# The sums of the first query half: two key tiles added on GpSimd, one late product with ones, and a new order of small DMAs

## The reference

```
qkv = clip(xn @ Wqkv.T, -8, 8);  q, k = layer_norm(q), layer_norm(k)
scores = q k^T / sqrt(32) + slope[h] * (j - i), causal
out = softmax(scores) @ v @ Wout.T
ffn = xn @ (alpha * sign(W)).T + bias
```

## Time and profile before

| | us |
|---|---|
| median of 3 runs | 1409.92 (1408.61 to 1413.5) |
| profiled execution, its own time | 1414.06 |
| its span, first to last instruction | 1412.3 |
| TensorE busy | 1341.1 (95%) |
| VectorE busy | 791.2 (56%) |
| ScalarE busy | 512.0 (36%) |
| GpSimd busy | 446.0 (32%) |
| TensorE's granted clock, mean | 0.993 of full |

### The profile page before, as it was taken

One profiled execution on the slowest core, in us unless ns is written; L12 is line 12 of the kernel. 1 busy time (PEld: TensorE's weight loads), 2 busy tenths in 40 slices (PEclk: granted clock), 3 DMA queues, 4 the chain that ended last, 5 costly groups with the idle time before them and its releaser, 6 DMA issues.

```text
span 1412.3 us, 36370 instructions
## 1 busy us (share of the span) xinstructions
PE 1341.1 (95%) x15012; PEld 678.3 (48%) x15012; DVE 791.2 (56%) x1794; ACT 512.0 (36%) x1019; POOL 446.0 (32%) x313
## 2 busy tenths in 40 slices
PE   5799999999999999699999999989999999999998
PEld 2344444444454444244345555555555555444443
DVE  4677266655566661112578778878877788201111
ACT  5444111111111110000037767767777777700000
POOL 1222000000000000000005555555544445697665
PEclk9999999999999999899999999999999999999999
DMA  5445122223222225712122333332333332144543
GB/s 214 156 158 198 70 53 67 67 72 77 61 74 67 70 71 134 195 68 81 54 62 57 90 87 81 89 79 79 84 89 87 87 87 60 46 170 136 165 148 119
DMA packets 143799, 137.99 MB, mean 98 GB/s; under 512 B 81969, under 2 KB 110769, under 8 KB 143474
## 3 DMA queue, kind: packets, MB, share of 16 engines
q1 hardware_dynamic: 79199, 99.55, 23.3%
q10 hardware_dynamic: 64467, 36.50, 10.1%
HBM read 93.42 MB, written 42.21 MB: 96 GB/s over the span
## 4 chain that ended last, share of the span: by engine, by line
PE 77%; DMA 9%; DVE 6%; issue 3%; ACT 2%; SPq 2%; POOL 0%; DVEq 0%; ACTq 0%; POOLq 0%
PE ps L1029 49%; PE ps L1099 7%; PE ps L1160 6%; DMA arena<-arena 5%; PE ps L1183 5%; PE ps L1188 4%; DVE ps L931 2%; PE ps L1076 2%; PE ps L1163 1%; DMA arena<-q_scr 1%; SPq L357 1%; PE ps L1193 1%; DMA v_scr<-arena 1%; ACT arena L663 1%; PE ps L1018 1%
## 5 line engine op out<-in xcount | busy, mean ns | idle before, releaser
L1029 PE MATMUL ps<-arena 128*128 128x512 f16 x3584 | 792.7, 381 | 17.9 <-DVE arena L890 11.8
L1029 PEld LDWEIGHTS ps<-arena 128*128 128x128 f16 (+1 forms) x3584 | 348.8, 98 | 437.2 <-issue 17.3
L740 ACT ACTIVATE arena<-ps 128x512 f32<-128x512 f32 (+3 forms) x768 | 339.6, 498 | 146.0 <-PE ps L1163 92.9
L599 POOL TENSOR_TENSOR arena<-arena 128x2048 f32<-128x2048 f32 (+1 forms) x48 | 201.8, 4204 | 390.8 <-ACT arena L740 388.4
L931 DVE CUSTOM_DVE_ANT_0 ps<-ps,arena 128x128 f32<-128x128 f32 (+3 forms) x512 | 239.4, 518 | 58.2 <-PE ps L1099 56.0
L1160 PE MATMUL ps<-arena 128*32 128x512 f16 (+3 forms) x3072 | 255.3, 327 | 4.0 <-ACT arena L740 2.5
L1099 PE MATMUL ps<-arena 127*32 127x512 f16 (+3 forms) x3072 | 237.3, 327 | 14.7 <-DVE arena L931 10.2
L648 ACT ACTIVATE arena<-arena 128x512 f32 (+1 forms) x64 | 40.1, 629 | 492.2 <-DMA arena<-in_wqkv_t 317.0
L890 DVE TENSOR_SCALAR arena<-ps 128x1024 f32<-128x1024 f32 x48 | 58.8, 1225 | 216.9 <-PE ps L1029 187.6
L935 DVE TENSOR_REDUCE arena<-ps 128x1 f16<-128x512 f32 x256 | 162.9, 682 | 15.7 <-PE ps L1099 15.7
L1183 PE MATMUL ps<-arena 128*32 128x512 f32 (+3 forms) x1536 | 160.8, 485 | 0.5 <-issue 0.3
(11 more groups left out here) (53 smaller groups left out, 785.9 us busy)
## 6 DMA issues: line engine op xcount, KB each, us to landing
arena<-in_x SPq DMA_DIRECT2D x32, 512.0 KB, 5.3
arena<-in_wqkv_t SPq DMA_DIRECT2D x48, 256.0 KB, 2.9
arena<-k_scr ACTq DMA_DIRECT2D x39, 256.0 KB
base_scr<-arena SPq DMA_DIRECT2D x16, 512.0 KB, 2.9
v_scr<-arena SPq DMA_DIRECT2D x16, 512.0 KB, 2.9
arena<-r_scr SPq DMA_DIRECT2D x32, 256.0 KB
arena<-base_scr SPq DMA_DIRECT2D x16, 512.0 KB, 4.4
out_dram<-arena SPq DMA_DIRECT2D x16, 512.0 KB, 6.2
```

What stands on the lines that cost most here:

```text
L599: nc.gpsimd.tensor_tensor(acc[:, :, at:HALF], former, p32[k % PSLOTS][:, :, 0:w], ALU.add)\
L740: nc.scalar.activation(p32[k % PSLOTS][:, j, 0:w], ps[:, TRB[x % RB], 0:w], ACT.Exp, scale=SCALE).then_inc(exp_done, 1)
L1029: ins = nc.tensor.matmul(dst[c], lhs(k, a), wparts[:, k, b, c * HALF:(c + 1) * HALF], start=(k == 0 and (a, b) == order[0]), stop=(k == KT ...
```

## The change

Chunks 1 and 2 of each group lose their products with ones, and so does chunk 0. GpSimd adds the slots of chunks 1 and 2 into chunk 0's slot (`add_first`), once TensorE has multiplied chunk 0 with V. `sums_first`, after the third score set of chunk 6, multiplies that slot with ones; chunk 3 keeps its own product and opens the bank. Since chunk 0's slot is kept longer, the slots are given by a table (`SLOT`, with `HELD` for the chunk that had the slot before), and chunk 3 shares a slot with chunk 2, chunk 11 with chunk 10. The sums of the first half are copied on their own (`sums0_copy`). On SyncE the next group's maxima row goes ahead of the previous half's reciprocals. The reciprocals stand at items 18 and 33 instead of 22 and 32, the stack loads at chunks 1 to 8 and V's at chunk 9, and `NATS`, `PV_AFTER` and the places of `o_norm`, `o_low`, `o_high` have new numbers.

```diff
         st_done = sem("st_done")
         exp_done = sem("exp_done")
         add_done = sem("add_done")
+        add0_done = sem("add0_done")
+        sums0_done = sem("sums0_done")
         pv_done = sem("pv_done")
         o_out = sem("o_out")
         s_out = sem("s_out")
...
             at = max(0, P * t - HALF * qb)
             return qb, t, at, HALF - at
-        NATS = [3, 4, 3, 4, 2, 5, 3, 4, 5, 3, 3, 3]
+        NATS = [3, 4, 3, 4, 3, 4, 4, 4, 5, 3, 2, 3]
         assert sum(NATS) == ITEMS
-        PV_AFTER = {(0, 2): [-2], (2, 1): [-1], (3, 0): [0], (4, 2): [1], (5, 2): [2], (6, 2): [3],
+        PV_AFTER = {(0, 2): [-2], (2, 1): [-1], (3, 0): [0], (4, 2): [1], (5, 2): [2], (5, 3): [3],
...
         def due(c, j):
...
         ADDED = (1, 2, 3, 5)
-        DIRECT = [qb == 0 or t not in ADDED for qb, t in CHUNKS]
+        DIRECT = [t not in (ADDED if qb else (0, 1, 2)) for qb, t in CHUNKS]
         ADDS = len(ADDED) - 1
+        ADDS0 = 2
+        FIRST_ADDS = {3: [1, 2]}
+
+
+
+        SLOT = [(0, 0), (1, 0), (2, 0), (2, 2 * P), (3, 0), (1, 0), (2, 0), (0, 0), (3, 0), (1, 0), (2, 0), (2, 2 * P)]
+
+
+        HELD = [-5, -3, -2, -1, -4, 1, 3, 0, 4, 5, 6, 6]
+
+        def slot(c):
+            i, col = SLOT[c]
+            return p32[i][:, :, col:col + span(c)[3]]
         def adds_for(k):
             n, c = k // NC, k % NC
-            return 0 if DIRECT[c] else ADDS * n + max(1, ADDED.index(CHUNKS[c][1]))
+            return ADDS * n + max(1, ADDED.index(CHUNKS[c][1])) if CHUNKS[c] in [(1, t) for t in ADDED] else 0
+
+        def adds0_for(k):
+
+            n, c = k // NC, k % NC
+            return ADDS0 * n + min(c, ADDS0) if 0 < c <= QB_END[0] else 0
         V_FIRST = NT - 4
...
                 row_b_in(n)
                 if n > 0:
                     sums_out(blk_no(n - 1, 1))
-                    recips_in(blk_no(n - 1, 1))
                 if n < GROUPS - 1:
                     row_a_in(n + 1)
+                if n > 0:
+                    recips_in(blk_no(n - 1, 1))
                 sums_out(blk_no(n, 0))
                 recips_in(blk_no(n, 0))
...
                 if t == ADDED[1]:
                     need(pool, pv_done, n * NC)
                 need(pool, add_done, adds_for(k) - 1)
-                former = p32[(k - 1) % PSLOTS] if t == ADDED[1] else acc[:, :, at:HALF]
-                nc.gpsimd.tensor_tensor(acc[:, :, at:HALF], former, p32[k % PSLOTS][:, :, 0:w], ALU.add)\
-                  .then_inc(add_done, 1)
+                former = slot(c - 1) if t == ADDED[1] else acc[:, :, at:HALF]
+                nc.gpsimd.tensor_tensor(acc[:, :, at:HALF], former, slot(c), ALU.add).then_inc(add_done, 1)
+
+            def add_first(n, c):
+
+                at = span(c)[2]
+                k = n * NC + c
+                pool.wait_ge(exp_done, GH * (k + 1))
+                pool.wait_ge(pv_done, n * NC + 1)
+                need(pool, add0_done, adds0_for(k) - 1)
+                total = slot(0)[:, :, at:HALF]
+                nc.gpsimd.tensor_tensor(total, total, slot(c), ALU.add).then_inc(add0_done, 1)
             for n in range(GROUPS):
                 for c in range(NC):
-                    if not DIRECT[c] and CHUNKS[c][1] > ADDED[0]:
+                    if CHUNKS[c] in [(1, t) for t in ADDED[1:]]:
                         add_in(n, c)
+                    for first in FIRST_ADDS.get(c, []):
+                        add_first(n, first)
                     if n > 0:
-                        if c == 1:
+                        if c == 0:
                             o_norm(n - 1, 0)
-                        if c == 4:
+                        if c == 5:
                             o_low(n - 1, 0)
                         if c == 7:
                             o_norm(n - 1, 1)
...
                 x = GH * k + j
                 w = span(c)[3]
                 if j == 0:
-                    need(act, pv_done, k - PSLOTS + 1)
-                    need(act, add_done, adds_for(k - PSLOTS))
+                    former = n * NC + HELD[c]
+                    need(act, pv_done, former + 1)
+                    need(act, add_done, adds_for(former))
+                    need(act, add0_done, adds0_for(former))
+                    if c == SLOT[1:].index(SLOT[0]) + 1:
+                        act.wait_ge(sums0_done, n + 1)
                 act.wait_ge(st_done, x + 1)
-                nc.scalar.activation(p32[k % PSLOTS][:, j, 0:w], ps[:, TRB[x % RB], 0:w],
+                nc.scalar.activation(slot(c)[:, j, :], ps[:, TRB[x % RB], 0:w],
                                      ACT.Exp, scale=SCALE).then_inc(exp_done, 1)
             def os_copy(n, qb):
...
                 act.wait_ge(pv_done, n * NC + QB_END[qb] + 1)
                 need(act, ol_done, m - 1)
                 nc.scalar.activation(os_sb[m % 2][:, 0, :], ps[:, O_BANK, :], ACT.Copy).then_inc(o_out, 1)
-                nc.scalar.activation(os_sb[m % 2][:, 1, :], ps[:, S_BANK, :], ACT.Copy).then_inc(s_out, 1)
+                if qb == 1:
+                    nc.scalar.activation(os_sb[m % 2][:, 1, :], ps[:, S_BANK, :], ACT.Copy).then_inc(s_out, 1)
+
+            def sums0_copy(n):
+
+                act.wait_ge(sums0_done, n + 1)
+                nc.scalar.activation(os_sb[0][:, 1, :], ps[:, S_BANK, :], ACT.Copy).then_inc(s_out, 1)
             def o_high(n, qb):
...
                     for j in range(GH):
                         exps(n, c, j)
                         if n > 0:
-                            if (c, j) == (2, 0):
+                            if (c, j) == (2, 1):
                                 o_high(n - 1, 0)
                             if (c, j) == (2, 1):
                                 os_copy(n - 1, 1)
-                            if (c, j) == (10, 3):
+                            if (c, j) == (11, 0):
                                 o_high(n - 1, 1)
-                            if (c, j) == (2, 3) and n < GROUPS - 1:
+                            if j == 3 and 0 < c <= LOADS and n + 2 < GROUPS:
+                                load_part(act, n + 2, c - 1)
+                            if (c, j) == (LOADS + 1, 3) and n < GROUPS - 1:
                                 if n == 1:
                                     for s in range(2):
                                         act.wait_ge(v_st[s], stored(NT // 2))
                                 load_vg(act, n + 1)
-                            if j == 3 and 3 <= c < 3 + LOADS and n + 2 < GROUPS:
-                                load_part(act, n + 2, c - 3)
                         if (c, j) == (6, 2):
                             os_copy(n, 0)
+                        if (c, j) == (6, 2):
+                            sums0_copy(n)
             os_copy(GROUPS - 1, 1)
             o_high(GROUPS - 1, 0)
             o_high(GROUPS - 1, 1)
...
                         nat_item(n + 1, pos)
                     elif pos == 0:
                         row_out(n, use(GROUPS, 0), row_b, rowb_ld)
-                    if pos == 22 and n > 0:
+                    if pos == 18 and n > 0:
                         recips(n - 1, 1)
-                    if pos == 32:
+                    if pos == 33:
                         recips(n, 0)
             def c_out_step(t, p):
...
                 n, c = k // NC, k % NC
                 qb, t, at, w = span(c)
                 first, last = t == 0, c == QB_END[qb]
-                p, v = p32[k % PSLOTS], vg[n % 2]
+                p, v = slot(c), vg[n % 2]
                 pe.wait_ge(exp_done, GH * (k + 1))
                 if first:
                     need(pe, o_out, blk_no(n, qb))
...
                     return ps[j * DH:(j + 1) * DH, bank, at:HALF]
                 for j in range(GH):
-                    ins = nc.tensor.matmul(dst(O_BANK, j, at), v[:, t, j, :], p[:, j, 0:w], start=first, stop=last)
-                if first:
-                    need(pe, s_out, blk_no(n, qb))
+                    ins = nc.tensor.matmul(dst(O_BANK, j, at), v[:, t, j, :], p[:, j, :], start=first, stop=last)
                 if DIRECT[c]:
+                    opens = first if qb else t == ADDS0 + 1
+                    if opens:
+                        need(pe, s_out, blk_no(n, qb))
                     for j in range(GH):
-                        ins = nc.tensor.matmul(dst(S_BANK, j, at), ones_w, p[:, j, 0:w],
-                                               start=first, stop=last and qb == 0)
+                        ins = nc.tensor.matmul(dst(S_BANK, j, at), ones_w, p[:, j, :], start=opens, stop=False)
                 if last and qb == 1:
                     pe.wait_ge(add_done, ADDS * (n + 1))
                     for j in range(GH):
                         ins = nc.tensor.matmul(dst(S_BANK, j, 0), ones_w, acc[:, j, :], start=False, stop=True)
                 ins.then_inc(pv_done, 1)
+            def sums_first(n):
+
+
+                pe.wait_ge(add0_done, ADDS0 * (n + 1))
```

(7 more changed lines are left out.)

2 lines of the change are left out of this document (1 added, 1 removed).

## The result

| | before | after |
|---|---|---|
| median of 4 runs each, same chip, us | 1411.71 (1408.61 to 1417.46) | 1376.3 (1375.31 to 1378.39) |
| profiled execution, its own time, us | 1414.06 | 1375.31 |
| its span, us | 1412.3 | 1373.5 |

The ratio is 0.9747, with a 95% interval from 0.9711 to 0.9782: 35 us less. The forecast was 1379 us with a range of 1370 to 1395, and 0.93 for faster.

A forecast was written before the change was run, and what follows sets the result against it. TensorE's work was taken to bound a group, with waits from VectorE's reciprocal stall on top. Terms -16 - 9 - 4 - 3 + 1 = -31 us took the profiled 1414.06 to about 1383, median 1379 us, range 1370 to 1395.

The forecast's parts named there:

- the signs named at the end of the prediction: Groups of 30.2 to 30.6 us, reciprocal waits under 5 us, prompt sums DMA, no q_scr wait, GpSimd busy 23 us.
- The products: TensorE's fp32 products with ones: net -1.07 us a group, counted in 15 groups, -16.0 us.
- The stall at the reciprocal: VectorE's wait for the first half's sums DMA, costing TensorE 10.2 us; its removal was put at -9 us.
- the small gaps: Gaps between TensorE's next products for the maxima that no row calls a wait: 0.3 us a group, -4 us.
- the quiet group: The group of 31.67 us in the profile before, read as bounded by TensorE's work; VectorE still held 1.54 us.
- The change takes four steps out of this chain: Previous half's reciprocal, broadcast, maxima row, sums on SyncE's queue; reciprocal from item 22 to 18 was to come 4.1 us earlier.
- The stack loads: Loads from q_scr issued two chunks, some 5 us, earlier; TensorE's 3.0 us of waits for them go: -3 us.
- GpSimd's adds: Two new adds, together 5.8 us, ending at 997.1 before ScalarE's chunk 6 exponentials; chain charged +1 us, bounds 0 and 7.5.
- the ring of three score banks covers this: ScalarE's waits of 0.3 and 0.2 us at chunks 5 and 6 hidden; TensorE needs the bank over 1 us later.
- The rival that ends slower: Adds take the path, holding ScalarE, copies, sums' DMA and reciprocal; decides from 3.3 us lag, 1413 with 3.5; chance 0.04.
- the stall at the other reciprocal: Second half's sums land late at item 18, VectorE stands 1.2 us, TensorE loses 0.9 a group: 1392 us; chance 0.14.
- line 941 caught: VectorE's minimum over two halves held by GpSimd's last add, 0.4 us a group: 1385 us; within the forecast's 0.66.

The follow-up runs named there:

- the lag of 1.24 us: Kernel after with three small GpSimd multiplications (112 columns, nothing waits for them) ahead of the two adds in each group: 1393.5 us, ratio 0.9875.
- With 2.6 us: Kernel after with six such small GpSimd multiplications ahead of the two adds in each group: 1433.66 us, ratio 1.0159.

## Why the prediction was right, and where its steps were not

**Direction, time and group length.** The direction came out, the time is 1376.3 us for 1379, and a group's mean 30.12 us for 30.4. Against the profiled execution of before the sum was -31 us, and it is -38.8 there. Of the signs named at the end of the prediction all but one are there: no group of 33 us or more among the 14, the reciprocal waits gone from them, line 475 issued at once, no wait for q_scr, GpSimd busy 23.12 us. The one that isn't: groups of 30.2 to 30.6 us were forecast, and most last 30.02. Of the signs against it one is there in small: TensorE's waits name ScalarE, 0.8 us in three places, all behind 1176 us. That the time came within 3 us is in part luck. The terms came out as other sizes than forecast, the forecast set out from a median of 1409.92 us where the runs beside the kernel after have 1411.71, and the next points show that the total is nearer than the terms deserve.

**The products: right.** -1.07 us a group was forecast and 0.97 measured (30.99 to 30.02). But the term can't be added to the kernel before: by itself it brings 5 us with an interval that holds zero. My sum treated the parts as independent. The runs give -5 (products), -22 (order and loads) and -35 together, so 8 us are there only when both are; in the profiled execution of the products alone 5.1 us of them are the clock's.

**The stall at the reciprocal and the small gaps, -9 and -4 (with the loads -16 in all): too small.** Order and loads give -22.4. The step that failed is the reading of the quiet group as "bounded by TensorE's work" at 31.6 us. Its busy time holds some 0.5 us in which products were still running and the next ones came late, at three products for the maxima right behind the reciprocal wait; the same work takes 30.99 us. So the small gaps were 31.6 - 31.0 = 0.6 us a group, where I had 0.3. Together with the 13.8 us of waits that I counted, 14 x 0.6 = 8.4 gives 22.2, which is what the order and the loads bring (22.4 by the medians, 21.5 over the 14 groups). The cause was named rightly; its size was read too small.

**"The change takes four steps out of this chain": too many.** The chain was right, since the issue now follows the copy within 0.03 us. But SyncE's order, undone alone, changes nothing, and the items, undone alone, cost 4.8 us. The late product makes the sums early enough in half the groups even with the old items and loads (11.3 us in 7 places instead of 29.3 in 13). They are several remedies for one stall, and I had added up their effects. Which of them is enough without the late product stays open beyond this: the loads alone are not, and the order and the loads together are.

**The stack loads, -3: the term that was mis-sized most.** I priced the loads at the wait that they caused in groups of 33 us, 3.0 us in all. Alone they bring nothing, since the reciprocal takes over what they release. In groups of 30 us their absence costs 21 us, 18.5 of it TensorE's waits for them. The wait of a resource that comes at a fixed place in the queue was read at a pace that the change itself was to raise.

**GpSimd's adds, +1: right in size, wrong in its cover.** I worked out that the second add ends 997.1 - 988.57 = 8.5 us after the group's head. It ends at 913.80 + 2.38 - 907.10 = 9.1: the first starts 0.3 us later than worked out, and between two adds that depend on each other lie 0.17 us. ScalarE waits for both adds, 0.24 us for the first and about 0.4 for the second, where 0.3 and 0.2 had been worked out, and in the first 13 groups TensorE has no wait for ScalarE. The step that failed is "the ring of three score banks covers this": of the 0.9 to 1.1 us of cover that I gave to it, the lag of 1.24 us found 0.11. I had looked for the cover behind the second add and the exponentials of chunk 6. It runs out behind the first: the exponential of chunk 5 starts at 913.72 and takes 0.59 us, and the score set that needs its bank starts at 914.50, 0.19 us after its end; its weight loads had begun at 914.37, after a wait of 0.17 us for the same exponential.

**The rival that ends slower: the mechanism is real, and its point was put too far.** It was to decide from a lag of 3.3 us. With 2.6 us the groups that pay only for the lag have lost 2.4 of the 2.47 us a group that the change gave (32.59 - 30.12), and the run as a whole is 1.6% slower than before, 17 us of the rest being the clock's (last section). By the price of the lag alone the break-even lies near 2.6 us, and below it where the clock falls. I was right to hold it unlikely, but with less margin than I believed.

**The last group, 0: -2.0.** The late product and GpSimd's part of the end were left out because the group is paced by others. The move of its last copy, which I had not costed at all, gives 1.7 of the 2.0 us.

**Line 941: priced nothing, and nothing in most groups.** The two rivals that have the stall at the other reciprocal or line 941 caught did not come. In the kernel after, line 985 was caught once in 14 groups (1.23 us), took 0.30 us in the next and 0.17 or 0.18 in the twelve others. That group's VectorE and GpSimd rows, and those of a group that got by:

```profile
963.23 1.23 DVE L985 TENSOR_TENSOR arena<-arena 128x16 f16<-128x16 f16 x1
```

```profile
963.27 1.17 POOL L609 TENSOR_TENSOR arena<-arena 128x512 f16<-128x512 f32 x1
```

```profile
903.18 0.17 DVE L985 TENSOR_TENSOR arena<-arena 128x16 f16<-128x16 f16 x1
```

```profile
903.25 1.20 POOL L609 TENSOR_TENSOR arena<-arena 128x512 f16<-128x512 f32 x1
```

In both it begins about 0.1 us before GpSimd's last add ends (963.32 and 903.32) and 0.04 to 0.07 us before the row of the operation behind it. Once it waited until 963.27 + 1.17 = 964.44, and the group lasted 30.57; at all other times it went ahead of that operation. The start alone doesn't decide it, since other groups got by with 0.03 us, and in the kernel with order and loads alone the minimum began 0.4 us before the add's end, took 0.41 to 0.47 us in every group, up to the add's end, and still went ahead of the operation behind. What decides it no run here shows; it happened once in this trace, and not in the 14 groups of the kernels with SyncE's order or the last copy's place put back. The shorter group does bring the minimum under GpSimd's last add, as the prediction had it, and it costs next to nothing there because that add is ending. What the Trainium skill states (SBUF — State Buffer, Who interferes with whom) agrees with the rows where the two overlap for long: the minimum, with two SBUF inputs, is held to the end of GpSimd's operation, here and in the kernel with one add, and the reciprocal of 914.89, with one, takes 0.25 us in the midst of an add that runs from 913.80 to 916.18.

## What to carry to other kernels

A wait in the trace of before is a price at the pace of before. For everything that comes at a fixed place (a load at a chunk, a DMA behind a queue entry), work out how long it takes and how much later it may come once the loop is shorter: moving the loads was worth nothing in the old kernel and 21 us in the new one.

Before reading the quietest period as an engine's own work, hold the count of its instructions and its busy time against what their sets take: busy time with gaps inside hid 0.6 us a group here, and laying two groups side by side, product by product, showed where they were. And where an estimate hangs on cover, the test that settles it is a few small operations put ahead of the suspect: three of them showed that 0.1 us was hidden where 0.9 to 1.1 had been worked out, and that the tight place was another than the one looked at.
